# Loading and splitting the first expert's weights while the router runs

## What the kernel computes

```
route_prob = softmax(xf @ Ws + bs).T            # 8 experts x 2048 tokens
route_vals, routes = top_k(route_prob, k)       # k = 256 in layer 0, 512 in layer 1
h   = gelu(xf[routes] @ W1 + b1)                # W1: 8 x 512 x 2048
out = (h @ W2 + b2) * route_vals                # W2: 8 x 2048 x 512
final = zeros.at[routes].add(out)
```

## Time and profile before

| | |
|---|---|
| median of three runs | 4181.79 us |
| the profiled execution | 4189.89 us |
| its span in the profile | 4188.3 us |
| PE, matmuls | 3748.4 us busy (89% of the span) |
| DVE | 2555.5 us (61%) |
| ACT | 2014.6 us (48%) |
| POOL | 1739.5 us (42%) |
| 16 DMA engines, queue of SP | 35.5% of the span |

### The profile page before, as it was taken

How to read it: one execution, slowest core, us unless ns; L and a number is a source line. 1 busy time by engine, 2 the same in 40 slices (tenths; PEclk the granted TensorE clock), 3 DMA queues, 4 the chain that set the end, 5 groups by cost and what they waited for, 6 DMA issues and landing times. The chain is left out here.

```text
span 4188.3 us, 77504 instructions
## 1 busy us (share of the span) xinstructions
PE 3748.4 (89%) x30860; PEld 2629.4 (63%) x30860; DVE 2555.5 (61%) x3210; ACT 2014.6 (48%) x3511; POOL 1739.5 (42%) x854
## 2 busy tenths in 40 slices
PE   7989799999999996649996699999997649999997
PEld 5768456666666563448995355555553438888886
DVE  4345778888888772566664677777772564433342
ACT  2222266666666662036662366666663024444442
POOL 0000287778777872001110488888884001111110
PEclk9999799999999998669998799999999659999999
DMA  4478624442444223236663522232202233333341
GB/s 161 169 247 284 182 61 106 103 112 63 105 103 112 58 65 117 101 134 205 210 188 111 146 77 77 78 81 78 77 22 80 98 105 120 115 113 113 113 117 29
DMA packets 287917, 485.16 MB, mean 116 GB/s; under 512 B 22289, under 2 KB 117521, under 8 KB 285585
## 3 DMA queue, kind: packets, MB, share of 16 engines
q1 hardware_dynamic: 272016, 443.00, 35.5%
q0 software_dynamic: 14080, 37.76, 3.9%
q10 hardware_dynamic: 1536, 0.40, 0.0%
HBM read 350.67 MB, written 130.02 MB: 115 GB/s over the span
## 5 line engine op out<-in xcount | busy, mean ns | idle before, releaser
L844 DVE TENSOR_REDUCE attn_parts<-attn_mx 128x4 f32<-128x2048 f32 x538 | 1232.6, 2291 | 378.3 <-PE attn_mx L686 378.0
L803 ACT ACTIVATE attn_probs<-attn_low 128x512 f32<-128x512 f32 (+1 forms) x2368 | 1235.1, 595 | 473.0 <-PE attn_low L714 353.2
L665 POOL TENSOR_TENSOR attn_psums<-attn_psums,attn_probs 128x1024 f32<-128x1024 f32 x536 | 1275.2, 2379 | 70.0 <-ACT attn_probs L803 4.8
L714 PE MATMUL attn_low<-attn_queries,attn_keys 97*128 97x256 f32 (+1 forms) x4736 | 917.7, 312 | 13.6 <-ACT attn_probs L803 5.2
L714 PEld LDWEIGHTS attn_low<-attn_queries,attn_keys 97*128 97x128 f32 x4736 | 660.7, 190 | 373.3 <-ACT attn_probs L803 188.8
L731 PE MATMUL attn_low<-attn_probs,attn_values 128*32 128x256 f32 x9472 | 632.2, 385 | 1.4 <-ACT attn_probs L803 1.4
L1462 DVE TENSOR_TENSOR ffn_wL<-ffn_raw,ffn_wH 128x2048 fp32r<-128x2048 f32 x128 | 293.4, 2292 | 224.2 <-ACT ffn_wH L1417 222.9
L1417 ACT ACTIVATE ffn_wH<-ffn_raw 128x2048 fp32r<-128x2048 f32 x128 | 245.2, 1916 | 339.1 <-DMA ffn_raw<-in_L_ffn_W_dram 178.3
L662 POOL TENSOR_TENSOR attn_psums<-attn_probs 128x1024 f32<-128x1024 f32 x88 | 209.6, 2382 | 380.0 <-ACT attn_probs L803 380.0
L731 PEld LDWEIGHTS attn_low<-attn_probs,attn_values 128*32 128x32 f32 x9472 | 248.2, 109 | 183.8 <-issue 3.9
L1374 PE MATMUL ffn_up<-ffn_xH,ffn_wH 128*128 128x256 f32 (+1 forms) x1024 | 350.6, 342 | 2.7 <-DVE ffn_xL L1468 2.7
(11 more groups left out here) (196 smaller groups left out, 4457.2 us busy)
## 6 DMA issues: line engine op xcount, KB each, us to landing
ffn_raw<-in_L_ffn_W_dram SPq DMA_DIRECT2D x128, 1024.0 KB, 5.6
attn_keys<-l_cross_keys SPq DMA_DIRECT2D x96, 512.0 KB, 6.8
attn_queries<-l_queries SPq DMA_DIRECT2D x48, 512.0 KB, 4.8
l_cross_keys<-projc_high SPq DMA_DIRECT2D x64, 256.0 KB
l_cross_keys<-projc_lowp SPq DMA_DIRECT2D x64, 256.0 KB
l_cross_values<-projc_vout SPq DMA_DIRECT2D x64, 256.0 KB
attn_keysn<-l_cross_keys SPq DMA_DIRECT2D x16, 1024.0 KB, 5.1
attn_values<-l_cross_values SPq DMA_DIRECT2D x32, 512.0 KB, 6.7
```

What stands on the lines that cost most here:

```text
L665: pool.tensor_tensor(ps, ps, at, ALU.add).then_inc(added, 1)
L714: mm = pe.matmul(out[:, n0:], KS[b][0:3 * HD + 1, h, kb * P:(kb + 1) * P], QS[b][0:3 * HD + 1, h, job.qb * QB + n0:(job.qb + 1) * QB], sta ...
L803: act.activation(probs[:, m % RING, i // 2, heads, n0:], sc[:, item % SC, :].rearrange("p (h q) -> p h q", q=QB)[:, :, n0:], ACT.Exp, scal ...
L844: op = dve.tensor_reduce(into, seen, AX.X, ALU.max)
```

## The change

The ring of weight tiles and the six semaphores that go with it (four for arrivals, `high_made`, `low_made`) are taken out of `experts` and put into a phase of their own around `route` and `experts`. In `route`, SP issues the first expert's four W1 chunks at once. ACT, behind its exponential, copies three of them to their high parts as they land, and POOL, behind its iotas, subtracts to make the three low parts. In `experts`, ACT and DVE no longer split these three chunks, and SP starts with chunk 4. The fourth chunk is split where it was, at the head of the loop. Nothing is changed in what is computed.

```diff
+class WeightRing:
+    SLOTS, PART = 4, 4
+    def __init__(self, ph):
+        self.raw, self.high, self.low = (ph.sb(n, [P, self.SLOTS, self.PART * BLK], t)
+                                         for n, t in (("raw", F32), ("high", F32R), ("low", F32R)))
+        self.raw_in = [ph.sem(f"raw_in{n}") for n in range(self.SLOTS)]
+        self.high_made, self.low_made = ph.sem("high_made"), ph.sem("low_made")
...
                 pool.iota(tok[:, 1, :], pattern=[[1, NTILE]], base=0, channel_multiplier=0).then_inc(numbered, 1)
+                for m in range(ring.SLOTS - 1):
+                    pool.wait_ge(ring.high_made, m + 1)
+                    pool.tensor_tensor(ring.low[:, m, :], ring.raw[:, m, :], ring.high[:, m, :].bitcast(F32), ALU.subtract
+                                       ).then_inc(ring.low_made, 1)
+
+            @block.sync
+            def _(sp):
+                for m in range(ring.SLOTS):
+                    sp.dma_start(ring.raw[:, m, :].rearrange("p (t n) -> p t n", n=BLK),
+                                 w1[0:1, :, m * BLK:(m + 1) * BLK].rearrange("e (t p) n -> p (e t) n", p=P)
+                                 ).then_inc(ring.raw_in[m], DMA)
...
                 act.activation(prob[:, :, :], rest[:, :, :], ACT.Exp).then_inc(expd, 1)
+                for m in range(ring.SLOTS - 1):
+                    act.wait_ge(ring.raw_in[m], DMA)
+                    act.activation(ring.high[:, m, :], ring.raw[:, m, :], ACT.Copy).then_inc(ring.high_made, 1)
...
+                def body(e, last):
+                    for m in range(RING, CHUNKS):
+                        load(e, m)
                         if m == HALF + 1:
-
                             sp.wait_ge(down_read, e * ST + ST)
                             sp.dma_start(b2b[:, :], b2[bass.ds(e, 1), :].rearrange("e n -> (e n)")
                                          .partition_broadcast(P)).then_inc(b2_in, DMA)
+                    if not last:
+                        for m in range(RING):
+                            load(e + 1, m)
+                each(sp, body)
...
-                for m in range(AHEAD):
-                    split_high(0, m)
                 turned_high(0, first=True)
...
-                for m in range(AHEAD):
-                    split_low(0, m)
                 turned_low(0)
...
+        with Phase(nc, "ring0") as ph:
+            ring = WeightRing(ph)
+            route(nc, "route0", c, logits, k0, c["tanhg"][:, 2:3], index[0], weight[0], ring, L0_ffn_W1)
+            experts(nc, "ffn0", c, xn1, x1, index[0], weight[0], k0, L0_ffn_W1, L0_ffn_b1, L0_ffn_W2,
+                    L0_ffn_b2, ACT.Gelu_apprx_tanh, ring)
```

More of the change, by code:

```diff
@@ L1065, in _, with route @@
                 dve.wait_ge(copied, BLOCKS + 1)
-def route(nc, name, c, logits, k, gate, index, weight):
+class WeightRing:
[5 more added lines that the diff above has]
+        self.high_made, self.low_made = ph.sem("high_made"), ph.sem("low_made")
+def route(nc, name, c, logits, k, gate, index, weight, ring, w1):
     ST = k // P
@@ L1239, in _, with experts @@
                 link(dve.tensor_scalar(weight[:, :, :], wf[:, :, :], gate, None, ALU.mult))
-def experts(nc, name, c, xn, acc, index, weight, k, w1, b1, w2, b2, gelu):
+def experts(nc, name, c, xn, acc, index, weight, k, w1, b1, w2, b2, gelu, ring):
     ST, C = k // P, D // P
     UP = 2 if ST > 2 else 4
-    PART = 4
+    PART = ring.PART
     HALF = FT // PART
     CHUNKS = 2 * HALF
-    RING, GF = 4, 2 * BLK // k
+    RING, GF = ring.SLOTS, 2 * BLK // k
     AHEAD = RING - 1
@@ L1258, in experts @@
     with Phase(nc, name) as ph:
-        raw = ph.sb("raw", [P, RING, PART * BLK])
-        wH = ph.sb("wH", [P, RING, PART * BLK], F32R)
-        wL = ph.sb("wL", [P, RING, PART * BLK], F32R)
+        raw, wH, wL = ring.raw, ring.high, ring.low
         b1T = ph.sb("b1T", [P, P])
@@ L1278, in experts @@
         turn = [ph.ps(f"turn{n}") for n in range(2)]
-        (b1_in, b2_in, b1_turned, b1_ready, idx_ready, turned, x_high, xT_ready, high_made, low_made, raised,
+        (b1_in, b2_in, b1_turned, b1_ready, idx_ready, turned, x_high, xT_ready, raised,
          gelued, h_ready, lowered, summed, down_read, y_ready, out_ready, asked, added) = (
             ph.sem(x) for x in ("b1_in", "b2_in", "b1_turned", "b1_ready", "idx_ready", "turned", "x_high",
-                                "xT_ready", "high_made", "low_made", "raised", "gelued", "h_ready", "lowered",
+                                "xT_ready", "raised", "gelued", "h_ready", "lowered",
                                 "summed", "down_read", "y_ready", "out_ready", "asked", "added"))
-        raw_in = [ph.sem(f"raw_in{n}") for n in range(RING)]
+        raw_in, high_made, low_made = ring.raw_in, ring.high_made, ring.low_made
         gathered, scattered = (c["keep"].sem(f"{name}_{x}") for x in ("gathered", "scattered"))
@@ L1303, in _, with load @@
                 sp.dma_start(b1n, b1.rearrange("e (t p) -> (e t) p", p=P)).then_inc(b1_in, DMA)
[L1304 to L1315, removed]
+                def load(e, m):
+                    sp.wait_ge(low_made, e * CHUNKS + (m + 1))
+                    at = raw[:, m % RING, :].rearrange("p (t n) -> p t n", n=BLK)
+                    if m < HALF:
+                        sp.dma_start(at, w1[bass.ds(e, 1), :, m * BLK:(m + 1) * BLK]
+                                     .rearrange("e (t p) n -> p (e t) n", p=P)).then_inc(raw_in[m % RING], DMA)
+                    else:
+                        n = (m - HALF) * PART * P
+                        sp.dma_start(at, w2[bass.ds(e, 1), n:n + PART * P, :]
+                                     .rearrange("e (t p) n -> p (e t) n", p=P)).then_inc(raw_in[m % RING], DMA)
+                def body(e, last):
+                    for m in range(RING, CHUNKS):
+                        load(e, m)
                         if m == HALF + 1:
@@ L1548, in program @@
                   L0_ffn_Ws, L0_ffn_bs, logits)
-        route(nc, "route0", c, logits, k0, c["tanhg"][:, 2:3], index[0], weight[0])
-        experts(nc, "ffn0", c, xn1, x1, index[0], weight[0], k0, L0_ffn_W1, L0_ffn_b1, L0_ffn_W2, L0_ffn_b2,
-                ACT.Gelu_apprx_tanh)
+        with Phase(nc, "ring0") as ph:
[3 more added lines that the diff above has]
+                    L0_ffn_b2, ACT.Gelu_apprx_tanh, ring)
         project(nc, "proj1", c, x1, T, D, True, [(L1_xattn_Wq, L1_xattn_bq, l1_queries)], [])
@@ L1557, in program @@
                   L1_ffn_Wr, None, logits)
-        route(nc, "route1", c, logits, k1, c["tanhg"][:, 3:4], index[1], weight[1])
-        experts(nc, "ffn1", c, xn3, out, index[1], weight[1], k1, L1_ffn_W1, L1_ffn_b1, L1_ffn_W2, L1_ffn_b2,
-                ACT.Gelu)
+        with Phase(nc, "ring1") as ph:
+            ring = WeightRing(ph)
+            route(nc, "route1", c, logits, k1, c["tanhg"][:, 3:4], index[1], weight[1], ring, L1_ffn_W1)
+            experts(nc, "ffn1", c, xn3, out, index[1], weight[1], k1, L1_ffn_W1, L1_ffn_b1, L1_ffn_W2,
+                    L1_ffn_b2, ACT.Gelu, ring)
 INPUTS = ['x', 'ctx_512', 'g_xattn', 'g_ffn', 'L0_xattn_Wk', 'L0_xattn_bk', 'L0_xattn_Wq', 'L0_xattn_bq',
```

## The result

The changed kernel takes 4193.57 us (median of 18 runs), the one before 4182.76 us (18 runs): ratio 1.0026, 95% interval [1.0019, 1.0034], slower by 10.8 us (7.9 to 14.2 us by the interval). The forecast was 4194.7 us, +12.9 us, with a range of 4180 to 4203 us. Single executions of one kernel spread over some 17 us, and the profiled one of the changed kernel was the shortest of them (4187.1 us; its router starts 9.5 us earlier than in the profile of before, ahead of everything that the change touches). So the two profiles are compared stage by stage and not by their spans. This table is worked out from the timelines: the route stage from DVE's first reduction to its copy of the index, the start of the experts from that copy to the first product.

A forecast was written before the change was run, and what follows sets the result against it. DVE's chain was taken to set the route stage's length, and waits for gather and splits the experts' start. Gain -10.7, barriers +0.8 and stalls +22.8 gave +12.9 us: 4194.7 us from the median 4181.8, range 4180 to 4203 us.

The forecast's parts named there:

- The gain: Start of the experts: without the splits the first product comes 5.9 and 4.8 us earlier, together 10.7 us.
- the 1 us allowed: Start of the experts: the gather may land up to 1 us earlier or later per layer, gain 8.7 to 12.7 us.
- The barriers: End of the ring's phase, twice: one more barrier of 0.4 us each, 0.8 us in all, bounds 0 to 3.
- The stall: Route stage: POOL's three subtractions shut out DVE's two-tile operations, 11.4 us per layer, 22.8 us in all.
- The mirrored reading: Gather issues waited for DVE's wL in 14 meetings; the reverse, POOL's subtraction shutting out DVE, was assumed to hold.
- rival A: Route stage: POOL does not hold DVE, only gain and barriers remain; -9.9 us, 4171.9 us; chance 18%.
- The order: Router rounds: cand stalls 3.5 us, then above 4.5 us, then cand 3.4 us, in each layer.
- Rival B: Route stage: DVE's two-tile operations run at half speed beside POOL, 5.8 us per layer; +1.7 us, 4183.5 us; chance 12%.
- Rival C: Route stage: waiting POOL always loses to DVE, 10.3 us per layer; +10.7 us, 4192.5 us; within the forecast's 70%.
- the gather's landing: Start of the experts: the gather's end was left at 1839.13 and 3421.82, with other weight loads issued beside it.

The follow-up runs named there:

- e2: Changed kernel with each of POOL's three subtractions cut into four pieces of 512 columns; route stages 83.3 and 93.0 us (one profile).
- e3: Changed kernel with POOL's three subtractions held back until the first one-hot rows are made; route stages 89.1 and 96.1 us (one profile).
- e5: Changed kernel with POOL copying raw to low instead of subtracting; route stages 78.6 and 88.8 us (one profile).
- e6: Changed kernel with POOL filling low with zeros instead of subtracting; route stages 76.2 and 85.8 us (one profile).
- e10: Changed kernel, but POOL makes only the first low part, in six released pieces, DVE the others behind xL; chunk 4 waits for the gather; 4164.98 against 4179.93 us.
- e4: The gather-alone run: changed kernel with SP holding chunks 4 to 6 until the gather has landed; first product at 9.8 and 14.8 us (one profile).
- e1: Changed kernel without POOL's three subtractions, DVE making the low parts at the start of the experts; 4173.99 against 4180.9 us, ratio 0.9983.

## Why the prediction was right

**The gain.** 5.9 and 4.8 us were predicted, 5.5 and 5.2 measured, 10.7 us both times in sum. The length of the chain behind the gather, taken from its second pair of turns, came out within 0.04 us (3.89 predicted, 3.85 measured in layer 0; 6.12 and 6.08 in layer 1); what differs is when the gather landed, +0.4 and -0.3 us, inside the 1 us allowed. That the two sums agree to 0.1 us is luck: the gather lands up to 1.3 us later in e2, e3, e5 and e6, whose experts start in the same way.

**The barriers.** 0.4 us each from the difference of two pauses; 0.44 us measured.

**The stall.** The mirrored reading of the earlier trace rows held, but the earlier trace rows did not show it. In the same trace `wL` began 12 times while a gather's issue was under way, 0.24 to 0.98 us after its start, and took 2.29 us as always:

```profile
1858.53 0.95 POOL L1332 DMA_INDIRECT ffn_xg<-xn,ffn_idx  x1 [25.27 <-DVE ffn_idx L1457]
...
1859.04 2.29 DVE L1462 TENSOR_TENSOR ffn_wL<-ffn_raw,ffn_wH 128x2048 fp32r<-128x2048 f32 x1 [1.29 <-issue]
```

Taken by themselves these rows speak for rival A, and the prediction does not weigh them. An issue that had begun did not hold DVE, POOL's subtraction did, and the trace of before could not tell that the two differ. Whether it is because an issue reads its indices only at its start is not shown.

The order was the predicted one (`cand`, `above`, `cand`, because POOL's next subtraction takes its turn behind the 0.19 us of `cand`), and the sizes too: 3.4, 4.2 and 3.0 us of surplus beside 3.5, 4.5 and 3.4. Of the 0.7 us in excess for each layer 0.2 us is POOL's subtraction, 4.51 us and not 4.57, three times. Some 0.4 us more is that I took the whole wait as surplus. A held operation ends sooner behind POOL than it would take by itself: the first `cand` of layer 0 waits from 1752.32 to 1755.86, 3.54 us, and ends 0.05 us later, so it is longer by 3.40 us and not by 3.54; the other two lose 0.14 us in the same way. The order depends on when the first copy is ready: in the gather-alone profile, layer 1 had `above`, `cand`, `above` and a stage of 97.4 us.

**The rivals.** Rival A (free reserve) fell with the stalls; it describes the kernel with fills on POOL, whose two stages sum to 195.0 us instead of 204.4: 8.5 us less with the barriers, where rival A had 9.9. Rival B was priced too high: at half speed a round takes 2.96 us, 4.6 rounds fit into POOL's 13.7 us, and they lose 4.1 us in each layer and not 5.8, so the rival stood at -1.8 us, 4180.0 us, still no change. It (sharing in small pieces) fell with `cand`'s surplus of 3.4 us in one operation of 0.19, and with e10, where a piece in a gap costs nothing. Rival C (POOL, waiting, always loses to DVE) is not what happened in the rounds, where `above` waited for POOL's second subtraction, but e3's layer 1 shows that POOL can be starved.

**What was not foreseen** lay outside the forecast: where I left the gather's landing untouched, it had some 3.5 us to give in each layer (e4). And the obvious repair, the subtractions back on DVE, meets the very exclusion that I had used for the router: the first turns move from 9.7 and 12.1 us to 10.8 and 15.9 (e1).

**The sum.** Stages and barriers give +11.6 us where the forecast had +12.9: 1.4 us less of stall, 0.1 us more of barriers. The runs' +10.8 us (7.9 to 14.2) does not tell the two apart.

## What to carry to other kernels

An idle POOL is no free reserve for arithmetic on SBUF while DVE runs a chain of operations on two SBUF tiles: in these rounds whichever started first held the other until it ended, so a long POOL instruction stops a chain of short DVE ones for nearly all its time. Cut the POOL work to the length of DVE's waits and release each piece by the DVE instruction ahead of the wait; and keep long two-tile DVE instructions away from indirect DMA issues that something waits for. When a transfer is what a stage waits for, hold back the loads beside it that nobody needs yet.

## What the runs showed of the hardware that was not expected

- The exclusion shows as duration of the instruction that waits, for DVE as for POOL, not as idle time: `above` 4.93 us instead of 0.69, the gather's issue 2.91 us instead of 1.0 (e1).
- It is not the same in both directions for every POOL instruction: a subtraction held DVE's operations on two SBUF tiles until it ended, a gather's issue under way did not (12 times `wL` at 2.29 us).
- `hot` (one f16 tile and a column of scalars in SBUF, bf16 out) is shut out by POOL's reading as well (up to 4597 ns, shortest 273), and an unbroken row of it kept a POOL instruction out for some 29 us in layer 1, while POOL came in at once in layer 0. `tokf`, with one f32 tile, was held too (2.08 us), and `passed` and `kth` were not.
- A semaphore that POOL raises behind an indirect DMA issue did not wait for it: DVE, which waited for that semaphore, began at 1820.51, the issue at 1820.88, and in layer 1 DVE began ahead of three of the four issues. Why is not shown.
